# First layer's routed experts: from every row to the picked rows, sorted, in tiles of 128

## The reference

```python
up_s = jnp.einsum('th,seh->tse', xt, shared_up)                     # 2 shared experts, 256 -> 128
shared = jnp.einsum('tse,she->th', jax.nn.gelu(up_s, approximate=False), shared_down)
probs = jax.nn.softmax(xt @ router_w.T, axis=-1)                    # 16 routed experts
topk_p, topk_i = jax.lax.top_k(probs, TOP_K)                        # TOP_K = 4
gate = jnp.zeros_like(probs).at[jnp.arange(xt.shape[0])[:, None], topk_i].add(topk_p)
up_r = jnp.einsum('th,reh->tre', xt, routed_up)
act = jax.nn.gelu(up_r, approximate=False) * gate[:, :, None]
routed = jnp.einsum('tre,rhe->th', act, routed_down)
return (shared + routed).reshape(b, s, h)
```

## Time and profile before

| | us |
|---|---|
| median of 3 runs | 4918.7 (4917.7 to 4920.89) |
| the profiled execution, span | 4926.8 |
| PE busy | 4323.7 (88%) |
| DVE busy | 3821.4 (78%) |
| POOL busy | 3039.8 (62%) |
| ACT busy | 2518.1 (51%) |

### The profile page before, as it was taken

How to read it: one execution, slowest core, us unless ns; L and a number is a source line. 1 busy time by engine, 2 the same in 40 slices (tenths; PEclk the granted TensorE clock), 3 DMA queues, 4 the chain that set the end, 5 groups by cost and what they waited for, 6 DMA issues and landing times. The chain is left out here.

```text
span 4926.8 us, 58327 instructions
## 1 busy us (share of the span) xinstructions
PE 4323.7 (88%) x18862; PEld 2818.8 (57%) x18862; DVE 3821.4 (78%) x6108; ACT 2518.1 (51%) x4753; POOL 3039.8 (62%) x1970
## 2 busy tenths in 40 slices
PE   5789999999999999998989899888988988499994
PEld 1355555555555655565655555555555555388883
DVE  6898788778778878775149988888988898555676
ACT  1244334334333433433468777777777777155552
POOL 3355555555554545554157888888888888555552
PEclk7799999999999999999999999999999999599997
DMA  4233332333332333332112112111222111486787
GB/s 145 78 106 109 105 97 90 110 98 112 101 107 88 102 106 102 103 109 97 37 62 86 69 71 71 66 69 68 91 79 74 68 65 68 161 244 203 260 272 279
DMA packets 302510, 545.46 MB, mean 111 GB/s; under 512 B 30593, under 2 KB 146561, under 8 KB 293249
## 3 DMA queue, kind: packets, MB, share of 16 engines
q1 hardware_dynamic: 274560, 466.08, 29.1%
q0 software_dynamic: 27648, 75.67, 4.3%
HBM read 422.71 MB, written 118.92 MB: 110 GB/s over the span
## 5 line engine op out<-in xcount | busy, mean ns | idle before, releaser
L1444 POOL TENSOR_TENSOR c_dbx<-c_dtx,c_Brep 128x1024 f32<-128x1024 f32 x512 | 1201.6, 2363 | 196.8 <-DVE c_hs L1462 99.2
L876 POOL TENSOR_TENSOR a_kv<-a_rk,a_kv 128x512 f32<-128x512 f32 x512 | 807.7, 1590 | 385.8 <-DMA a_kv<-v_rows 385.7
L1462 DVE TENSOR_TENSOR_SCAN c_hs<-psum,c_carry,c_dbx 128x512 f32<-128x512 f32 x768 | 937.7, 1267 | 121.0 <-ACT psum L1451 71.8
L802 POOL TENSOR_TENSOR a_hid_e<-a_hid_e,a_g_rep 128x512 f32<-128x512 f32 x256 | 387.2, 1515 | 826.4 <-ACT a_hid_e L791 648.6
L1451 ACT ACTIVATE psum<-c_dt,c_cols 128x512 f32<-128x512 f32 x1024 | 697.3, 688 | 368.7 <-DVE c_hs L1462 362.9
L885 DVE TENSOR_TENSOR_SCAN a_S<-a_decay,a_carry,a_kv 128x513 f32<-128x513 f32 x512 | 792.9, 1549 | 102.6 <-POOL a_kv L876 98.5
L1478 PEld LDWEIGHTS psum<-ident,c_hs 128*128 128x128 f32 x4096 | 489.7, 145 | 394.3 <-DVE c_hs L1462 215.7
L1478 PE MATMUL psum<-ident,c_hs 128*128 128x128 f32 x4096 | 613.8, 283 | 109.5 <-DVE c_hs L1462 106.7
L891 DVE TENSOR_TENSOR a_prod<-a_rk,a_S 128x512 f32<-128x512 f32 x512 | 576.3, 1126 | 80.5 <-PE psum L907 80.4
L783 PE MATMUL psum<-a_W_down,a_hid_e 128*128 128x256 f32 x2304 | 549.9, 384 | 60.6 <-DVE a_carry L883 35.5
L207 PE MATMUL psum<-a_xT,a_W_up 128*128 128x512 f32 x1152 | 563.7, 619 | 25.2 <-ACT a_hid_e L791 14.1
(11 more groups left out here) (266 smaller groups left out, 6868.9 us busy)
## 6 DMA issues: line engine op xcount, KB each, us to landing
a_kv<-v_rows SPq DMA_DIRECT2D x512, 256.0 KB
a_g_rep<-g_rows SPq DMA_DIRECT2D x256, 256.0 KB, 4.0
c_Brep<-b_rows SPq DMA_DIRECT2D x64, 1024.0 KB, 4.6
d_xs<-sorted_rows SPq DMA_DIRECT2D x320, 128.5 KB
d_w<-results SPq DMA_DIRECT2D x64, 512.0 KB, 11.5
d_w<-in_d_experts SPq DMA_DIRECT2D x32, 768.0 KB
sorted_rows<-d_zeros SPq DMA_DIRECT2D x66, 128.5 KB, 11.9
a_xa<-in_L_attn_x SPq DMA_DIRECT2D x16, 512.0 KB, 4.7
```

Of the source, the lines that this page charges most:

```text
L802: hid[e - 1] = m_done["gate used", n] = pool.mark(nc.gpsimd.tensor_tensor(hid_e[:, r, :], hid_e[:, r, :], g_rep[:, n % NG, :], ALU.mult))
L876: m_kv[g] = pool.mark(nc.gpsimd.tensor_tensor(kv[:, g % NV, 1:C + 1], rk[slot][:, 1, hb, :], kv[:, g % NV, 1:C + 1], ALU.mult))
L1444: m_dbx[g] = m_dbx[g + 1] = pool.mark(nc.gpsimd.tensor_tensor(dbx[:, r:r + 2, :], dtx[slot][:, e, :].unsqueeze(1).broadcast_to([P, 2, C]), ...
L1462: m_scan[q] = dve.mark(nc.vector.tensor_tensor_scan(hs[:, q % NR, :], psum[:, DA + q % ND, :], dbx[:, q % NX, :], first, ALU.mult, ALU.add))
```

## The change

A row's four picks are now computed and nothing else. Per chunk, `expert_inputs` also counts the rows that picked each expert (products with a triangle and with ones), and places each pick: the row number in a list in memory that has a room for each of the 16 experts. `scatter(c)` copies each row with its 16 gates (272 numbers) to its four places: 16 indirect DMAs a chunk on POOL (L892). After four chunks, a segment, `plan` makes from the counts the tables of tiles: 79 tiles of 128 rows for each of the four segments, whatever the counts are. Zero blocks are written behind the rooms' filled parts. `tiles()` fetches a tile's rows (SP, L929), transposes them, multiplies by the expert's weights (found by a register), Gelu, transposes, multiplies, scales by the gate on ACT (L1004) and stores the result (SP, L935). `combine(c)` loads the stored chunk again, half by half through the buffer `xc` (in the last segment whole, through `xb`), and adds the four results of each row by indirect DMAs that gather and add (POOL, L1048, 16 a chunk), then stores it again (SP, L1056). The two shared experts are computed like a small feed-forward (`dense`). One transposed input `xT` is left where there were two. `PACE` is 4400.

The diff, cut to its core:

```diff
-        k = e - 1 - SH
-        if 0 <= k < E:
-            r = (e - 1) % NHE
-            while not is_done(("gates", c)):
-                yield
-            pool.after(hid[e - 1])
-            n = c * E + k
-            pool.engine.wait_ge(s_grep[n % NG], 16 * (n // NG) + 16)
-            hid[e - 1] = m_done["gate used", n] = pool.mark(nc.gpsimd.tensor_tensor(hid_e[:, r, :], hid_e[:, r, :], g_rep[:, n % NG, :], ALU.mult))
-            if k >= 1 and k - 1 + NG < E:
-                fetch_gate(c, k - 1 + NG)
...
+    m_gates = dve.mark(nc.vector.tensor_tensor(row[:, :, D:], prob[:, :, :], R["total"][:, :].unsqueeze(2).broadcast_to([P, TL, E]), ALU.mult))
+    yield from rest(1)
+    i, bank = yield from G.claim(pe)
+    pe.after(m_ahead)
+    m = pe.mark(matmuls(nc, bank[:, 0:TL * E], [(tri[:, :], chosen[:, :, :].rearrange("p t e -> p (t e)")), (ones[:, :], ahead[:, 0:TL, :].rearrange("p t e -> p (t e)")),
+                                                (ones[0:1, :], base_row.unsqueeze(1).broadcast_to([1, TL, E]))]))
+    m_done["counted", c] = m
+    yield from rest(1)
     dve.after(m)
-    m = dve.mark(nc.vector.tensor_tensor(gates[:, :, :], gates[:, :, :], R["total"][:, :].unsqueeze(2).broadcast_to([P, TL, E]), ALU.mult))
+    m = G.freed[i] = dve.mark(nc.vector.tensor_tensor(others[:, :, :], bank[:, 0:TL * E].rearrange("p (t e) -> p t e", e=E), chosen[:, :, :], ALU.mult))
+    dve.after(m)
+    for t in range(TL):
+        m = dve.mark(nc.vector.max(R["best"][:, t, :], others[:, t, :]))
+    yield
+    dve.after(m)
+    dve.mark(nc.vector.tensor_copy(from_row[:, c, :].rearrange("p (t k) -> p t k", t=TL), R["best"][:, :, 0:TOP]))
+    m = dve.mark(nc.vector.tensor_copy(to_row[:, c % 2, :].rearrange("p (t k) -> p t k", t=TL), R["best"][:, :, 0:TOP]))
+    m_done["placed", c] = [m, m_gates, m_row]
...
+    for k in range(0, E, 4):
+        for at in numbers(of_pad, k, nc.sync.engine, Z.ROOMS * P - P):
+            nc.sync.dma_start(picked_rows[slot][bass.ds(at, P), :], I["picked_zeros"]).then_inc(s_pad, 16)
+        yield
+    m_done["plan", s] = m
...
+def scatter(c):
+    s = segment_of[c]
+    while not is_done(("placed", c)):
+        yield
+    while s >= 2 and not is_done(("tiles read", s - 2)):
+        yield
+    yield from rest(2)
+    pool.after_alone(*m_done["placed", c], m_done.get(("tiles read", s - 2)))
     for t in range(TL):
+        for k in range(TOP):
+            at = t * TOP + k
+            nc.gpsimd.indirect_dma_start(out=picked_rows[s % 2], in_=row[:, t, :], in_offset=None,
+                                         out_offset=bass.IndirectOffsetOnAxis(ap=to_row[:, c % 2, at:at + 1], axis=0),
+                                         bounds_check=Z.rows - 1).then_inc(s_rows[c % 2], 16)
+            yield
+    m_done["scattered", c] = True
...
+    def fetch(j):
+        if j % 4 == 0:
+            for k, v in enumerate(numbers(table, 2 * NT + j, nc.sync.engine, Z.ROOMS)):
+                at_row[j + k] = v
+        q = begun + j
+        sp.after(m_T.get(q - NTX), m_ty.get(q - NTX))
+        nc.sync.dma_start(t_rows[:, q % NTX, :], row_of[bass.ds(at_row.pop(j), 1), :, :].rearrange("a p d -> p (a d)")).then_inc(s_tx[q % NTX], 16)
+    def store(j):
+        q = begun + j
+        sp.after(m_ty[q])
+        nc.sync.dma_start(result_of[j], t_y[:, q % NTY, :]).then_inc(s_ty[q % NTY], 16)
+    for j in range(min(2, total)):
+        fetch(j)
+    held = {}
+    for step in range(total + 5):
+        if 0 <= step - 4 < total:
+            store(step - 4)
+        if step + 2 < total:
+            fetch(step + 2)
...
+        i, bank = yield from G.claim(pe)
+        pe.engine.wait_ge(s_tx[q % NTX], 16 * (q // NTX + 1))
+        for kb in range(KB):
+            m = nc.tensor.transpose(bank[:, kb * P:(kb + 1) * P], t_rows[:, q % NTX, kb * P:(kb + 1) * P], ident[:, :])
+        Columns.sent += KB * P
+        m_T[q] = pe.mark(m)
+        held["x"] = i, bank
+    if 0 <= step - 3 < total:
+        i, bank = held["hT"]
+        act.after(m_hx[q - 3], m_dn.get(q - 3 - NTH))
+        m_hT[q - 3] = G.freed[i] = act.mark(nc.scalar.copy(t_hT[:, (q - 3) % NTH, :], bank[:, 0:P]))
+    yield
+    j = step - 1
+    if 0 <= j < total:
+        if j % 4 == 0:
+            for k, v in enumerate(numbers(table, j, nc.tensor.engine, (E - 1) * KB * P)):
+                at_e[j + k] = v
+        i, bank = yield from G.claim(pe)
+        pe.after(m_xT[q - 1])
+        for kb in range(KB):
+            m = nc.tensor.matmul(bank[:, 0:P], t_xT[:, (q - 1) % NTT, kb * P:(kb + 1) * P], up_flat[:, bass.ds(at_e[j] + (SH * KB + kb) * P, P)],
+                                 start=(kb == 0), stop=(kb == KB - 1))
+        Columns.sent += 2 * KB * 200
+        m_up[q - 1] = pe.mark(m)
+        held["h"] = i, bank
+    if step < total:
+        i, bank = held["x"]
+        act.after(m_T[q], m_up.get(q - NTT))
+        m_xT[q] = G.freed[i] = act.mark(nc.scalar.copy(t_xT[:, q % NTT, :], bank[:, 0:D]))
+    yield
+    j = step - 3
+    if 0 <= j < total:
+        i, bank = yield from G.claim(pe)
+        pe.after(m_hT[q - 3])
+        m_dn[q - 3] = pe.mark(nc.tensor.matmul(bank[:, 0:D], t_hT[:, (q - 3) % NTH, :], down_flat[:, bass.ds(at_e.pop(j) + SH * D, D)], start=True, stop=True))
+        Columns.sent += 2 * D
+        held["y"] = i, bank
...
+def combine(c):
+    s, last_segment = segment_of[c], c >= opens[-1]
+    while not is_done(("tiles", s), ("out", c)) or c >= 1 and not is_done(("final", c - 2 if last_segment else c - 1)):
+        yield
+    pool.after(m_done["rows", s])
+    if c in opens or last_segment:
+        for i in range(NTY):
+            pool.engine.wait_ge(s_ty[i], 16 * len(range(i, m_done["tiles", s], NTY)))
+    if last_segment:
+        yield from with_picks(c, range(TL), xb[c % 2])
+    else:
+        yield from with_picks(c, range(0, TL // 2), xc)
+        yield from with_picks(c, range(TL // 2, TL), xc)
+    m_done["final", c] = s_final[c % 2], 16 * ended_sums[c % 2]
+begun_sums, ended_sums, xc_stored = [0, 0], [0, 0], []
+def with_picks(c, blocks, place):
+    side, part = c % 2, slice(blocks[0], blocks[-1] + 1)
+    sp.engine.wait_ge(s_store[side], 16 * (c // 2 + 1))
+    if place is xc:
+        for done in xc_stored[-1:]:
+            sp.engine.wait_ge(*done)
+    elif ended_sums[side]:
+        sp.engine.wait_ge(s_final[side], 16 * ended_sums[side])
+    begun_sums[side] += 1
+    loaded = 16 * begun_sums[side]
+    nc.sync.dma_start(place[:, :, :], chunk_of(chunks_out, c)[:, part, :]).then_inc(s_xc[side], 16)
     yield from rest(2)
+    pool.engine.wait_ge(s_xc[side], loaded)
+    for k in range(TOP):
+        for n, t in enumerate(blocks):
+            if k:
+                pool.engine.wait_ge(s_pick[side][t], 16 * (c // 2 * TOP + k))
+            at = t * TOP + k
+            nc.gpsimd.indirect_dma_start(out=place[:, n, :], out_offset=None, in_=picked_results[segment_of[c] % 2],
+                                         in_offset=bass.IndirectOffsetOnAxis(ap=from_row[:, c, at:at + 1], axis=0),
+                                         bounds_check=Z.results - 1, compute_op=ALU.add).then_inc(s_pick[side][t], 16)
+            yield
+    yield from rest(1)
+    for t in blocks:
+        sp.engine.wait_ge(s_pick[side][t], 16 * (c // 2 + 1) * TOP)
+    ended_sums[side] += 1
+    nc.sync.dma_start(chunk_of(chunks_out, c)[:, part, :], place[:, :, :]).then_inc(s_final[side], 16)
+    if place is xc:
+        xc_stored.append((s_final[side], 16 * ended_sums[side]))
...
+def block_work(c, quota):
+    fed, split, tiled = False, False, False
+    ff = sh = None
+    while not split or not tiled:
+        if ff is None and not fed and is_done(("h2T", c)):
+            ff = feed_forward(c)
+        if ff is not None:
+            if next(ff, "end") == "end":
+                ff, fed = None, True
+            yield
+        elif fed and sh is None and not split and is_done(("xT", c)):
+            sh = shared(c)
+        if sh is not None:
+            if next(sh, "end") == "end":
+                sh, split = None, True
+            yield
+        tiled = tiled or tiles_begun[0] >= quota
+        if not tiled:
+            tiled = next(tile_stream, "end") == "end"
...
-        PACE = 4800
+        PACE = 4400
...
+SEGMENTS = [4, 4, 4, 4]
+def __init__(self, chunk):
+    self.per_chunk = chunk * self.TOP // self.SLOTS
+    longest = max(self.SEGMENTS)
+    self.PITCH = longest * chunk // self.SLOTS + 1
+    self.width = 256 + self.EXPERTS
+    self.per_window = -(-self.tiles(longest) // longest)
+def tiles(self, chunks):
+    return chunks * self.per_chunk + self.EXPERTS - 1
+def quota(self, window):
+    if window >= sum(self.SEGMENTS):
+        return math.inf
+    return self.per_window * max(0, window - self.SEGMENTS[0])
```

396 lines of the change are left out of this document (249 added, 147 removed).

## The result

The changed kernel takes 5413.3 us (median of 4 runs, 5400.9 to 5416.0) where the kernel before takes 4918.2 us (4914.9 to 4920.9): 1.100 times as long, 95% interval 1.0987 to 1.1017. Forecast was slower, 5020 us, range 4840 to 5120. The direction came, the size did not: +495 us in place of +101.

The account below looks back on a forecast made before the run. PE was taken to bound the steady chunks, with DVE only 18 us of work behind. Scan phase -204 us and tail +305 us gave +101 us, a median of 5020 us, range 4840 to 5120.

Parts of the forecast that it names:

- Engine loads: First layer's scan phase, work per chunk: DVE about 110 us, PE 80 then 110 from window 5, POOL 86.
- A tile at 1.5 us of PE: PE work for one routed tile of 128 rows: 1.5 us, 20 tiles a window from window 5 on.
- The sum of the scan phase: First layer's scans: 123 us a chunk in windows 2 to 4, 131 in 5 to 15; 2049.5 us, saving 204.
- The tail: From the first layer's last product to the second layer's first scan: 535 us against 230.2, so +305 us.
- Opening with plan and zero blocks: Start of the tail: 168 us of leftover work up to segment 3's plan, then 20 us to the first rows.
- Tile stage: Last segment's 79 tiles: 33 held behind seven gather halves of 19.6 us (137 us), 46 free at 1.9 us (88 us).
- Last stage with its end: End of the tail: last four chunks' gathers at 1.28 us each on POOL, 107 us, then 10 to the first scan.
- The bound of the prediction: Upper bound of the tail: 600 us if accumulating gathers land 2 us later each.
- The price of an indirect DMA: POOL spends 1.02 us on a scatter or gather, 1.28 per tail gather; by the skill's fit 128 KB takes 2.3 us.
- Rival 1: Scan phase: DVE alone sets the pace, windows 2 to 15 at 117 us, total 4846 us; chance 0.23.
- Rival 2: Tail: tile fetches not held by SP, tile stage 148 us, tail 438, total 4923 us; chance 0.13.
- Rival 3: Scan phase: POOL held up, 2.3 us an indirect DMA, 140 us a chunk, +99 us, total 5119; chance 0.14.

Follow-up runs that it names:

- e1: Changed kernel without the routed tiles' fetches and their work on PE and ACT, zeros stored instead; scatters, plans and gathers stay; 5146.4 us.
- e3: Changed kernel without tiles, gathers and scatters; feed-forward, shared experts, routing, counting and plans stay; 4618.2 us.
- e4: Changed kernel with PACE, PE's allowance of columns a step, at 3800 in place of 4400; 5296.8 us, timed again 5325.1 us (ratio 1.0815).
- e10: e3 with PACE at 3800 in place of 4400; 4583.8 us.
- e8: Changed kernel with PACE at 5200 in place of 4400; 5447.6 us.
- after: The changed kernel itself, with nothing further altered; 5413.3 us, scan phase 2302 us and tail 665 us in its profile.
- e2: Changed kernel without the adding gathers and the loads and stores around them; scatters, plans and tiles stay; 5093.1 us.
- e6: Changed kernel with gathers that overwrite instead of adding, so the sums are left out; 5305.6 us.

## Why the prediction was wrong, and where it was right

**Engine loads: right.** DVE 110 us a chunk was forecast, 109.4 and 112.8 came. PE 80 in windows 2 to 4: 95.3 us at clock 0.79 is, as an estimate, 95.3 x 0.79/0.98 = 77 at the clock of before. POOL 86, came 85.2, but this is luck: there were 11 gathers a window and not 16, each scatter and gather cost more than forecast (1.42 and 1.93 us in place of 1.02), and the multiplies less (1457 ns in place of 1.6 us).

**A tile at 1.5 us of PE (bounds 1.2 and 1.9): it held.** Against e1 a tile adds 1.28 us to PE's busy time. Brought to the clock of before this is, as an estimate, (114.7 x 0.85 - 91.3 x 0.80)/(18.3 x 0.98) = 1.36 us.

**The sum of the scan phase: this step failed.** "When PE and DVE are equally full ... 110 + 13 = 123 us; for 5 to 15 ... 110 + 21 = 131". Chunk 1 was taken as the model of how two engines share a chunk, with no look at when in the chunk each has its work. Before, the routed experts of two chunks ago were there at every step to stand beside the scans; the change took them out and left feed-forward and shared experts, which follow from one another and come as one burst, at an allowance of 4400 columns a step. The tenths of chunk 3, e3, e4, e10 and, for the windows from 5 on, e8 show it: without routed work the window stays at 127 to 131; spreading the burst brings 133.1 to 123.6 and 151.2 to 138.7, and 130.6 to 122.8 without routed work. Windows 2 to 4 took 24 us more than the work of their fuller engine where the sum had 13. Of the 30 + 222 us that windows 2 to 4 and 5 to 15 missed by, e4 gives back 28 + 138, though 69 us of that return in its tail.

The second part of the same step is what the tiles add. The sum let 30 us of PE work lengthen a window by 8, 123 to 131. In after, against e1, 23.4 us of PE work lengthened it by 21.1; at 3800, e4 against e10, all the routed work lengthened it by 15.3 us with 16.4 us of PE work. So the 7.7 us a window that e4 does not give back are the 15.3 us in place of 8. The PE work of the tiles did not fit beside DVE's, although neither engine was over 76% busy. Which of the waits keeps it from fitting was not tested and stays open.

**The tail, 535 forecast, 665 measured: right mechanism, terms too small.** Opening with plan and zero blocks 188, came 247: PE was busy for 177 us, near the 168 of the forecast, and idle for 70, where 20 stood. In e2, without gathers, the last scatter comes 215 us after the scans' end (after: 219), so the gathers have no part in that; which of the chains of chunk 15 holds it was not tested. Tile stage 225 + 5, came 263: seven halves at 25.8 in place of 19.6 us give 43 by themselves; the free tiles came at (2857 - 2770)/46 = 1.9 us as forecast. Last stage with its end 117, came 155: 64 gathers at 1.86 in place of 1.28 give 37. The last comes nearly whole from the adding, which no row of before shows, the halves' to a good half: e6, without it, has a tail of 597 us, 68 less. The bound of the prediction ("land 2 us later each", 600 us) was short even so. It put the extra price on the landing, which was 1.0 us and not 2, and none on POOL's own time, and 59 us of the miss are the opening's, which it did not touch.

**The price of an indirect DMA.** The fit in the Trainium skill (DMA: Bandwidth & Descriptors, section "Anatomy of one DMA — SWDGE (gpsimd) path"), 2.0 us plus bytes/436 GB/s, gave 2.3 us for 128 KB as an estimate. Here a plain gather landed 2.8 us after its issue and an adding one 3.8, so the measured values decide. The third gather of the half shown did wait (1.1 us) where by the estimate it would not. The Trainium skill also says (SBUF — State Buffer, section "SBUF: two separate sides") that GpSimd's descriptors can starve beside VectorE. Scatters were slower beside a busy DVE: 1284 ns in the median, 1422 in the mean and 5530 at most in chunks 5 to 15, against 982 in the median in the tail, with DVE light. The slow ones stood beside scans, not copies: those mostly beside a scan took 1627 ns in the median. In the mean it was 0.4 us, not a factor of five, and POOL was not the bound of these windows. Whether they waited for descriptors is not shown.

**Rivals.** Rival 1 (DVE alone, 117 us) is out of reach in the mean even with no routed work and the lower allowance (123 in e10). Rival 2 (tail not held by SP) is refuted by the tail of after, with its tile fetches behind the halves' stores, and by e2, where a tile passes every 1.81 us without them. Rival 3 saw its sign, indirect DMAs over 1.3 us on POOL, and little of its effect: taking the gathers out gave 33 us of scan phase where the rival had 99.

## What to carry to other kernels

Two engines' loads in a stage do not give its time: cut one period into ten slices and see who is full in each, above all after taking out work that could run at any moment, because that work had filled the gaps between the other engine's bursts. When such work goes, the pacing numbers tuned with it (here the columns allowed a step) have to be tuned again: one constant was worth 1.9 points of the 10.0% lost. And loads in one stage do not simply hide behind one another while both engines look idle a quarter of the time: what the tiles added to PE they added to the window. Last, count every gather and store of a batched scheme as a serial chain behind its last batch: here 79 tiles, held back by the gathers of the batch before, and then 64 gathers with nothing beside them.

## What the runs showed of the hardware

An indirect DMA that adds cost GpSimd 1.55 us where a plain one took 1.02, and landed after 3.8 us where the plain one took 2.8 (after and e6). Beside a busy VectorE the scatters rose from 982 to 1284 ns in the median, the adding gathers from 1554 to 1852. In chunk 3 the granted clock was 0.50 and 0.52 in slices where PE was busy for 58% and 80% of the time, 0.87 where it was 63%, and 0.97 to 1.00 in the middle, where it was full. Raising it from 0.79 to 0.88 with idle products did not shorten the windows, with 21 us more of PE's work in each.
